# TensorE's wait for the output stores, in front of its branch over the general path, taken out

## What is computed

```python
h = jnp.maximum(_layernorm(x, axis=-1), 0.0)
H = h @ W_fc + b_fc
s_src = H @ w_att[:d]
s_dst = H @ w_att[d:]
scores = s_src[:, None] + s_dst[None, :] + b_att
scores = jnp.where(A > 0, scores, jnp.float32(NEG_INF))
alpha = jax.nn.softmax(scores, axis=1)
return x + alpha @ H
```

## Time and profile before

| | us |
|---|---|
| median of 3 runs | 179.26 |
| lowest and highest | 179.03 and 180.56 |
| the profiled execution | 178.96 |
| its span, first to last instruction | 177.0 |

### The profile page before, as it was taken

How to read it: one execution, slowest core, us unless ns; L and a number is a source line. 1 busy time by engine, 2 the same in 40 slices (tenths; PEclk the granted TensorE clock), 3 DMA queues, 4 the chain that set the end, 5 groups by cost and what they waited for, 6 DMA issues and landing times.

```text
span 177.0 us, 3000 instructions
## 1 busy us (share of the span) xinstructions
PE 154.3 (87%) x992; PEld 128.4 (73%) x992; DVE 120.2 (68%) x354; ACT 89.7 (51%) x257; POOL 10.3 (6%) x32
## 2 busy tenths in 40 slices
PE   0629959996959999999989999999699999989992
PEld 0327726765547686766667999998699999889982
DVE  0897595938899945989858846662597286655453
ACT  2569984999659234112336233346034345666641
POOL 2102602000050001000000000000000000000000
PEclk9999978999988999999999999999789999999999
DMA  5999999999999999999999999999999999999982
GB/s 147 400 446 420 415 446 426 429 422 433 426 433 426 416 433 429 420 426 437 420 419 426 422 426 428 422 427 417 428 425 428 420 408 411 408 406 410 402 335 69
DMA packets 9810, 71.64 MB, mean 405 GB/s; under 512 B 1089, under 2 KB 1858, under 8 KB 5570
## 3 DMA queue, kind: packets, MB, share of 16 engines
q1 hardware_dynamic: 9216, 71.18, 96.7%
q10 hardware_dynamic: 578, 0.26, 0.6%
HBM read 69.34 MB, written 2.10 MB: 404 GB/s over the span
## 4 chain that ended last, share of the span: by engine, by line
DMA 54%; PE 24%; DVE 12%; issue 4%; ACT 2%; SPq 2%; DVEq 0%; ACTq 0%
DMA ring<-adj 54%; PE bank L997 21%; DVE mask L608 6%; PE bank L1074 2%; DVE features L630 1%; DVE weighted L841 1%; ACT sums_T L529 1%; DVE mask L616 1%; PE bank L1063 1%; ACT weighted L432 1%; SPq L331 1%; DVE high_bits L709 1%; DVE sums_T L735 1%; PE bank L1133 1%; PE bank L1129 0%
## 5 line engine op out<-in xcount | busy, mean ns | idle before, releaser
L608 DVE TENSOR_SCALAR mask<-ring 128x1024 fp32r<-128x1024 int32 (+3 forms) x77 | 63.5, 842 | 38.4 <-DMA ring<-adj 35.5
L997 PE MATMUL bank<-features,mask 128*128 128x258 f32 x512 | 67.2, 290 | 3.0 <-DVE mask L608 2.9
L997 PEld LDWEIGHTS bank<-features,mask 128*128 128x128 f32 x512 | 64.1, 194 | 4.4 <-DVE mask L608 3.5
L518 ACT ACTIVATE mask<-ring,half_steep 128x512 fp32r<-128x512 int32 x49 | 33.5, 720 | 53.0 <-DMA ring<-adj 52.4
L970 PE MATMUL bank<-mask,features 128*128 128x512 f32 x128 | 39.5, 434 | 9.3 <-ACT features L438 4.5
L970 PEld LDWEIGHTS bank<-mask,features 128*128 128x128 f32 x128 | 24.9, 205 | 21.8 <-DVE mask L608 8.7
L975 PE MATMUL bank<-mask,features 128*128 128x512 f32 x128 | 36.5, 409 | 0.0
L975 PEld LDWEIGHTS bank<-mask,features 128*128 128x128 f32 x128 | 25.3, 198 | 6.1
L432 ACT ACTIVATE weighted<-relu,w_over_std 128x128 f32<-128x128 f32 x32 | 10.2, 393 | 3.9 <-DVE w_over_std L701 3.7
L742 DVE SCALAR_TENSOR_TENSOR x_sb<-bank,inv_den,x_sb 128x128 f32<-128x128 f32 x28 | 8.0, 344 | 5.6 <-PE bank L1050 3.9
L443 ACT ACTIVATE relu<-x_sb,neg_mean 128x128 f32<-128x128 f32 x32 | 9.8, 401 | 3.2 <-DVE neg_mean L639 3.2
(11 more groups left out here) (99 smaller groups left out, 94.2 us busy)
## 6 DMA issues: line engine op xcount, KB each, us to landing
ring<-adj SPq DMA_DIRECT2D x15, 2048.0 KB, 17.3
ring<-adj SPq DMA_DIRECT2D x15, 1536.0 KB, 13.3
ring<-adj SPq DMA_DIRECT2D x15, 512.0 KB, 8.9
ring<-adj SPq DMA_DIRECT2D x2, 1024.0 KB, 7.3
out<-x_sb SPq DMA_DIRECT2D x7, 256.0 KB, 7.4
ring<-adj SPq DMA_DIRECT2D x2, 768.0 KB, 11.8
x_sb<-x SPq DMA_DIRECT2D x1, 1024.0 KB, 20.4
x_sb<-x SPq DMA_DIRECT2D x2, 256.0 KB, 3.8
```

Of the source, the lines that this page charges most:

```text
L518: nc.scalar.activation(mask[:, n % MASKS, cols - part:cols], ring[:, n // 2 % RING, begin + cols - part:begin + cols], ACT.Sigmoid, bias=h ...
L608: nc.vector.tensor_scalar(mask[:, n % MASKS, 0:cols], ring[:, n // 2 % RING, begin:begin + cols], 0.0, None, ALU.is_gt).then_inc(masks_rea ...
L997: last = nc.tensor.matmul(bank[:, BANKS[g][b], 0:WIDE], mask[:, n % MASKS, at:at + P], features[:, t, :, :].rearrange("p h d -> p (h d)"), ...
```

## The change

One statement is removed: TensorE no longer waits for all stores to have landed before it branches on `flag`. ScalarE's wait for the same semaphore stays, and so does SyncE's in the general path.

```diff
             pe.wait_ge(path_chosen, 1)
             general = pe.value_load(flag[0:1, 0:1], min_val=0, max_val=1)
-
-            pe.wait_ge(out_stored, 16 * STORES)
             with pe.If(general != 0):
                 with pe.Fori(0, T) as s:
                     pe.wait_ge(gen_probs_ready, s + 1)
```

## The result

The changed kernel takes 180.21 us (median of 22 runs, 179.69 to 181.52), against 179.25 us for the kernel before (22 runs, 178.93 to 181.12). The two medians are 0.96 us apart. The ratio of the two kernels is 1.0041, with a 95% interval of 1.0021 to 1.006, which makes the changed one slower by about 0.7 us (0.4 to 1.1), where 0.45 us less was forecast. The time is within 1% of that before, and outside the forecast's range.

A forecast was written before the change was run, and what follows sets the result against it. The prediction took TensorE's slow branch behind the last stores' landing to bound the end. Removing the wait would save 0.45 us, from a 179.26 us median to 178.8 us, with other costs at nothing; range 178.3 to 179.8 us.

The forecast's parts named there:

- What bounds the end: At the closing barrier: TensorE arrives last because a 459 ns branch stands behind its wait; ScalarE has the same wait.
- The gain behind the landing: Behind the last store's landing: TensorE's branch is done early, ScalarE becomes last, and the end moves forward 0.45 us.
- The fetch of instructions: At TensorE's branch, moved to about 174.2 us: no code packet was thought to come with it; costed at nothing.
- rival (c): Around the span: the code packet after the span comes earlier, saving up to 1.3 us more, 177.5 us; chance 0.04.
- Rival (b): At the last stores: the early branch's code fetch delays their landing, end 0.85 us later, 180.1 us; chance 0.05.
- (a): At the closing barrier: nothing moves, ScalarE arriving when TensorE does now; 179.3 us; chance 0.14.
- (d): At TensorE's end: another wait for the stores still holds it, so no gain; counted within (a)'s chance.

The follow-up runs named there:

- one waiter: The kernel before without ScalarE's wait for all stores at its end, leaving TensorE's as the only one; 179.31 us, ratio 1.0004.
- wait behind: The changed kernel with TensorE's wait for all stores put back, but behind its branch; 180.15 us, ratio 1.0081 to the kernel before.
- wait for results: The changed kernel with TensorE waiting for VectorE's last result, not for any store, before its branch; 180.36 us, ratio 1.0055 to the kernel before.
- wait for one store: The changed kernel with TensorE waiting before its branch for the first of the four last stores alone; 178.91 us, ratio 0.9976 to the kernel before.

## Why the prediction was wrong

**What bounds the end: right.** TensorE was the last at the barrier for its slow branch, not for its wait. In the kernel before, ScalarE has the same wait and drains 0.4 us earlier; with the wait in place and half the branch's time gone, the two drains are 0.1 us apart. The kernel with one waiter adds that ScalarE's wait beside TensorE's costs nothing.

**The gain behind the landing: right in size.** With the branch early, or hidden in the flight of the last stores, and no packet in the way, the ratios are 0.9976 (twice) and 0.9981: 0.34 to 0.43 us, where 0.45 was forecast (0.21 to 0.42 us by the medians). The 0.46 us between the two drains came from rounded starts; unrounded, the trace has 176.82 - 176.40 = 0.42 us. In the changed kernel itself the end of the span came 177.8 - 177.4 = 0.4 us behind the last landing, against 0.8 before.

**The fetch of instructions: the step that failed.** It read that "the branch of before brought no such packet with it, though it took 459 ns, and I cost the fetch at nothing". The rows said that no packet came between 176 and 177.04 us, and I took the end of the branch for the end of what it sets off. The packet comes 1.2 us after the branch starts, at 177.4 us, behind the span. It had a row of its own, and rival (c) even discussed it and dismissed it with "it rather belongs to what follows the barrier". It was the only q8 packet there, and its start, 1.2 us behind the start of the branch, would have said whose it was. In its place the runs showed a term of 1.0 us on one DMA engine, which put the last landing at 177.4 us instead of 176.2 and turned a gain of 0.45 us into a loss of 0.7.

**Rival (b): it is what happened.** It had the price nearly right: 1.3 us of one engine, the stores ending at 177.5, a net 0.85 us and 180.1 us. Measured were 1.0 us of one engine, a release of ScalarE at 177.4, a net 0.7 us by the ratio (0.96 by the medians), and 180.21 us. Its point of decision, a fetch between about 173 us and the last packet of the stores, held in every run: packets at 175.3, 175.5 and 175.5 us cost, those behind the span didn't. The 0.05 that it got was the mistake. It was priced from rows, and I let a window that was 0.4 us too short speak against it. Only the wait of the rule cited there from the Trainium skill ("Runtime: NRT & Kernel Launch", section Instruction fetch mechanics), a fetch before execution goes on, didn't show: TensorE's drain came 0.8 us ahead of the packet.

**Rivals (a), (c) and (d): no.** TensorE's part went as forecast, with a branch of 363 ns in the changed kernel instead of 459; nothing around the span was saved, since 179.69 - 177.8 = 1.9 us is what it was.

**The range.** It ended at 179.8 us, just under rival (b), and so missed by 0.4 us. That the time stays within 1%, which had 0.95, held. The prediction took a gain of 0.25% for one that would read as none; the intervals here are 0.2 to 0.5% wide, and two of the three kernels with the gain stand clear of no change.

## What to carry to other kernels

A wait can protect something that it doesn't name, as here the last store. Before one is taken out, list what the instructions behind it set off, a jump's fetch of code too, and ask what is in flight at their new time; look for the effect of an instruction behind its end, up to the next microsecond or two and past the end of the span. A branch over a long path at the end of a kernel may be followed by a packet of code. Here the branch cost nothing when it was taken while the stores were in flight but late enough that the packet came after theirs (by a wait for the first of the last stores), or when the path was short enough that no packet came.

## What was not expected of the hardware

- A packet of code of 0.02 MB takes 1.0 to 1.4 us, and 9 packets of a store, one engine's share, start only as it ends: a 64 KB store lands after 3.1 to 3.6 us instead of 1.7 to 2.1 (three traces).
- The code packet starts 1.1 to 1.3 us after the branch does in five traces with it (before, changed, wait behind, wait for results, one waiter), and 1.7 us after it in the kernel with the wait for one store. Why it was later there is open.
- TensorE's branch takes 353 to 459 ns when the packet follows and 223 to 231 ns when none does. The same branch takes 45 to 76 ns on the other engines.
